# An attention loop between two layers of experts: the values' product taken for two blocks of queries at once, and the normalised input kept in memory

## The reference, cut to what matters

```python
x = x + 0.5 * _ffn_ref(_layernorm(x), controller, f1, bias, f2)
h = _layernorm(x)
Q, K, V = proj(h, Wq, bq), proj(h, Wk, bk), proj(h, Wv, bv)   # 16 heads of 64
rel_emb = rel_table[clip(i - j + 1023, 0, 2046)]
scores = (Q @ K.T + einsum('bhid,ijd->bhij', Q, rel_emb)) / 8
out = softmax(scores) @ V                                     # per head
x = x + out.transpose(0, 2, 1, 3).reshape(b, n, e) @ Wo.T + bo
x = x + 0.5 * _ffn_ref(_layernorm(x), controller, f1, bias, f2)
```

## Time and profile before

| | us |
|---|---|
| median of 3 runs | 3956.51 |
| lowest and highest | 3954.49, 4080.84 |
| the profiled execution | 3966.11 |
| its span, slowest core (core 1) | 3964.1 |
| spans of all cores | 3927.9 to 3964.1 |

### The profile page before, as it was taken

One profiled execution on the slowest core, in us unless ns is written; L12 is line 12 of the kernel. 1 busy time (PEld: TensorE's weight loads), 2 busy tenths in 40 slices (PEclk: granted clock), 3 DMA queues, 4 the chain that ended last, 5 costly groups with the idle time before them and its releaser, 6 DMA issues.

```text
span 3964.1 us, 80834 instructions; the slowest of 8 cores (3927.9 to 3964.1 us)
## 1 busy us (share of the span) xinstructions
PE 3500.4 (88%) x29664; PEld 2215.0 (56%) x29664; DVE 2097.3 (53%) x2703; ACT 1561.0 (39%) x2013; POOL 187.9 (5%) x289
## 2 busy tenths in 40 slices
PE   6988469999999999999999999999987789988842
PEld 4776134565566566566557557556654545567610
DVE  4333223666666666666666666666675733333311
ACT  3222122544554554554454454455454411122200
POOL 0000000000000000000000000000000000000001
PEclk8799687999999999999999999999998989999965
DMA  4557883564565565465466456456468711156697
GB/s 135 170 188 248 308 257 118 180 200 162 171 208 171 165 206 178 158 203 189 157 193 197 150 184 208 156 173 212 153 188 248 222 55 64 59 178 211 222 320 264
DMA packets 248833, 736.25 MB, mean 186 GB/s; under 512 B 16656, under 2 KB 66320, under 8 KB 240272
## 3 DMA queue, kind: packets, MB, share of 16 engines
q1 hardware_dynamic: 178448, 401.82, 30.7%
q0 software_dynamic: 63680, 317.74, 24.3%
q10 hardware_dynamic: 6336, 11.54, 1.3%
HBM read 405.05 MB, written 325.98 MB: 184 GB/s over the span
## 4 chain that ended last, share of the span: by engine, by line
PE 75%; DMA 13%; ACT 4%; issue 4%; DVE 3%; SPq 0%; POOL 0%; ACTq 0%; DVEq 0%; POOLq 0%
PE PS L158 65%; PE PS L155 10%; DMA out<-SCR 3%; DMA SCR<-f2r 3%; ACT SCR L981 3%; DMA xs<-SCR 3%; DMA SCR<-qsl 1%; DMA SCR<-x 1%; ACT SCR L919 1%; DVE SCR L978 1%; DVE SCR L888 1%; DMA qsl<-SCR 1%; DMA SCR<-itb 0%; DMA SCR<-xs 0%; DVE SCR L898 0%
## 5 line engine op out<-in xcount | busy, mean ns | idle before, releaser
L158 PE MATMUL PS<-SCR 128*64 128x128 f32 (+5 forms) x20928 | 3159.3, 393 | 282.9 <-DMA SCR<-itb 100.4
L158 PEld LDWEIGHTS PS<-SCR 128*64 128x64 f32 (+2 forms) x20928 | 1793.0, 167 | 1174.3 <-issue 1121.0
L888 DVE TENSOR_TENSOR SCR<-PS,SCR 128x1024 f32<-128x1024 f32 (+3 forms) x608 | 642.0, 1056 | 765.9 <-PE PS L158 730.8
L155 PEld LDWEIGHTS PS<-IDENT,SCR 64*128 64x128 f32 (+1 forms) x8736 | 456.5, 141 | 551.8 <-issue 528.6
L155 PE MATMUL PS<-IDENT,SCR 64*128 64x64 f32 (+1 forms) x8736 | 557.7, 236 | 159.2 <-ACT SCR L981 47.2
L898 DVE TENSOR_REDUCE SCR<-SCR 128x2 f32<-128x1024 f32 x512 | 622.5, 1216 | 26.7
L919 ACT ACTIVATE SCR<-SCR 128x2048 f32<-128x2048 f32 x256 | 510.7, 1996 | 122.8 <-DVE SCR L912 122.5
L802 ACT ACTIVATE SCR<-PS 128x1024 f32<-128x1024 f32 (+2 forms) x448 | 413.8, 924 | 259.6 <-PE PS L158 244.2
L981 ACT ACTIVATE SCR<-PS 128x1024 f32<-128x1024 f32 x256 | 262.5, 1025 | 363.8 <-PE PS L155 348.9
L978 DVE COPY SCR<-PS 128x1024 f32<-128x1024 f32 x256 | 311.1, 1215 | 24.9 <-PE PS L155 23.1
L943 ACT ACTIVATE SCR<-PS 128x128 f32<-128x128 f32 x128 | 35.6, 278 | 526.9 <-PE PS L155 517.3
(11 more groups left out here) (47 smaller groups left out, 616.6 us busy)
## 6 DMA issues: line engine op xcount, KB each, us to landing
qsl<-SCR SPq DMA_DIRECT2D x320, 512.0 KB, 4.8
itb<-SCR POOLq DMA_DIRECT2D x64, 1024.0 KB, 13.3
SCR<-itb SPq DMA_DIRECT2D x32, 2048.0 KB, 27.0
SCR<-f1p SPq DMA_DIRECT2D x64, 512.0 KB, 9.1
SCR<-f2r SPq DMA_DIRECT2D x64, 512.0 KB, 12.4
SCR<-qsl POOLq DMA_DIRECT2D x16, 2048.0 KB, 10.7
SCR<-qsl POOLq DMA_DIRECT2D x16, 1920.0 KB, 10.3
SCR<-qsl POOLq DMA_DIRECT2D x16, 1792.0 KB, 10.4
```

The lines of the kernel that those rows point to most:

```text
L155: return do("tensor", lambda e: e.matmul(out, lhsT, rhs, start=start, stop=stop, is_transpose=True), sig)
L158: return do("tensor", lambda e: e.matmul(out, lhsT, rhs, start=start, stop=stop), sig)
L888: e.tensor_tensor(sr(n, a0, [[1, w]]), pap(BK_C + a0 - j0, [[512, 2], [1, w]]), in1, ALU.add))
```

## The change

- **Values for two blocks.** `emit_pv` runs for odd blocks only and takes the block before along: 256 moving columns instead of 128, half of the groups. The transposed probabilities of the even block are kept whole (`PTE`, four groups), those of the odd one in two places (`PTO`). Reciprocals have a place for each of the two, and VectorE multiplies 256 columns at once.
- **h in memory.** h is laid out in four chunks of 512 rows (16 KB a partition each) and stored to `hts`. In the loop only two chunks are in SBUF; the projections of a pair go chunk by chunk (`order`), and after Q of its first and its second chunk `load_chunk` loads the other two in their places, in four transfers of 512 KB in the next four steps.
- **Q has two buffers**, so all 48 pieces of a pair run in the pair before.
- **Pieces** come in the order K, V, Q for each chunk. A step without a product of values has one piece, a step with one has one every second time.
- **Last results through memory.** The last pair's results go to `aofm` too. `prefetch` loads the first half (16 transfers) and the weights (16); the second half is loaded after the barrier, and the first two tiles of the output product start with the first half meanwhile.

The diff, cut to its core:

```diff
             for eng in Bld.ENGS:
-                barrier(eng)
+                barrier(eng, () if attn is None or eng in ("sync", "gpsimd")
+                        else ("aow", "aox"))
...
+
+                a_ld = []
+
+                def load_ao(part):
+                    for m in range(4, 8):
+                        tok = dma("sync",
+                                  ap(attn["aof"] + 2048 * m + 512 * part,
+                                     [[1, 512]]),
+                                  AP(aofm.tensor, 128 * m * S + 512 * part,
+                                     [[S, 128], [1, 512]]), LXS[part])
+                    a_ld.append(tok)
+
+                load_ao(0)
                 for t in range(2):
                     x_ld.append(dma("sync", ap(XT[t], [[1, 1024]]),
                                     src_hbm[128 * t:128 * (t + 1), :],
                                     ("xta", "xtb")[t]))
                 bo_ld = dma("sync", ap(BO, [[1, 1024]]), borep[:, :], "sx")
                 ct_ld = dma("sync", ap(CT, [[1, 1024]]), ctrlc[:, :], "ld")
+                for part in range(1, 4):
+                    load_ao(part)
             dma("sync", ap(FB, [[1, 32]]), f1bs[:, :], "ld")
...
+                o_k, o_t = {}, {}
+
+                def emit_o(t, ms):
+                    if ms[0] == 0:
+                        o_k[t] = next_pair()
+                        wt("tensor", pair_free[o_k[t]])
+                    if ms[-1] == 7 and t % 4 == 0:
+                        wt("tensor", a_ld[t // 4])
+                    for nb in range(2):
+                        bank = 1024 * o_k[t] + 512 * nb
+                        for m in ms:
+                            o_t[t] = mm(PS[:, bank:bank + 512],
+                                        ap(AOF + 2048 * m + 128 * t,
+                                           [[1, 128]]),
+                                        ap(WO[m] + 512 * nb, [[1, 512]]),
+                                        m == 0, m == 7,
+                                        sig=(nb == 1 and m == 7))
+
+
+                emit_o(0, range(4))
+                emit_o(1, range(4))
                 for t in range(NT):
-                    k = next_pair()
...
-            PT = (3072, 4096)
+            PTE, PTO = HBASE + 8192, (HBASE + 14336, HBASE + 15360)
...
-            QT = XA + 12288
+            QT = (XA + 12288, HBASE + 12288)
...
+            hbuf = [HBASE + 4096 * i for i in range(4)]
+            h_ready = [None] * 4
+            loads = []
...
+            def load_chunk(nb, done):
+
+                new, sem = (nb + 2) % 4, ("hca", "hcb")[nb % 2]
+                hbuf[new] = hbuf[nb]
+                h_ready[new] = (sem, b.cnt[sem] + 64)
+
+                def part(i, base=hbuf[nb]):
+                    if i == 0:
+                        wt("sync", done, hs_tok["a"], hs_tok["b"])
+                    dma("sync", ap(base + 1024 * i, [[1, 1024]]),
+                        hts[128 * new:128 * (new + 1),
+                            1024 * i:1024 * (i + 1)], sem)
+                loads.extend(lambda i=i: part(i) for i in range(4))
+
+            def pieces(p, j, nb):
+                last = j == 3 and p + 1 < NPAIR
...
-                        yield piece
+                for part in range(4):
+                    def piece(part=part):
+                        tok = proj_qk_piece(p, QT[p % 2], WQ, BQS, 0.125,
+                                            state["wq"], nb, part)
+                        if tok:
+                            state["q"][p % 2][nb] = state["pj"]
+                        if tok and last:
+                            wt("sync", tok)
+                            state["wq"] = load_w(wqt, WQ, p + 1, "wqa")
+                        if tok and p > 0 and j < 2:
+                            load_chunk(nb, tok)
+                    yield piece
...
+            def order(p):
+                return (2, 3, 0, 1) if p > 0 and p % 2 == 0 else (0, 1, 2, 3)
...
 
                 wt("tensor", z_tok[n], pv_free[0], rz_tok[0])
-                tok = mm(PS[:, BK_PV + 128:BK_PV + 256], ap(RB, [[1, 128]]),
+                rz = BK_PV + 256 + 128 * (n % 2)
...
-                slot = g % 2
+                dst = PTE + 1024 * g if n % 2 == 0 else PTO[g % 2]
                 eng = "vector" if g in (0, 3) else "scalar"
-                wt(eng, tok, pt_free[slot])
...
             def emit_pv(n, g):
                 p, q = n // 16, n % 16
-                wt("tensor", pt_tok[(n, g)], state["v"][p % 2])
+                even, odd = PTE + 1024 * g, PTO[g % 2]
+                wt("tensor", pt_tok[(n - 1, g)], pt_tok[(n, g)],
+                   state["v"][p % 2])
...
                     for h in range(2):
-                        tok = mm(pap(BK_PV, [[1, 128]], 64 * h, 64),
+                        tok = mm(pap(BK_PV, [[1, 256]], 64 * h, 64),
                                  ap(VT[p % 2] + 128 * kc + 64 * h, [[1, 64]]),
-                                 ap(PT[g % 2] + 256 * h + 64 * k,
-                                    [[512, 2], [1, 64]]),
+                                 ap(even + 256 * h + 64 * k,
+                                    [[odd - even, 2], [512, 2], [1, 64]]),
                                  kc == 0, kc == 15,
                                  sig=(k == 3 and h == 1))
-                pt_free[g % 2] = tok
+                pt_free[even] = pt_free[odd] = tok
...
-                        dst = AOF + 2048 * p + 128 * q
-                    elif q % 4 == 0:
+                    wt("vector", tok, rz_tok[0])
+                    dst = AOT + 512 * slot + 128 * (q % 4 - 1)
+                    if q % 4 == 1:
                         wt("vector", ao_tok[slot])
                     pv_free[0] = do("vector", lambda e: e.tensor_tensor(
-                        ap(dst, [[1, 128]]), PS[:, BK_PV:BK_PV + 128],
-                        ap(RZ, [[1, 128]]), ALU.mult))
-                    if q % 4 == 3 and n < LAST:
+                        ap(dst, [[1, 256]]), PS[:, BK_PV:BK_PV + 256],
+                        ap(RZ, [[1, 256]]), ALU.mult))
+                    if q % 4 == 3:
                         wt("gpsimd", pv_free[0])
...
+            def store_chunk(nb, which):
+                wt("gpsimd", h_ready[nb])
+                hs_tok[which] = dma(
+                    "gpsimd", hts[128 * nb:128 * (nb + 1), :],
+                    ap(HBASE + 4096 * nb, [[1, 4096]]), "hs" + which)
...
+                    todo.extend(pieces(0, t // 4, t // 4))
+                    if t >= 8:
+                        store_chunk(t // 4, "b")
...
+            store_chunk(0, "a")
+            store_chunk(1, "a")
+            wt("scalar", hs_tok["b"])
+            wt("vector", hs_tok["b"])
...
-                if i < 28:
+                if i < 16:
                     m, part = i // 4, i % 4
                     dma("scalar", ap(AOF + 2048 * m + 512 * part, [[1, 512]]),
                         AP(aofm.tensor, 128 * m * S + 512 * part,
                            [[S, 128], [1, 512]]), "af")
-                elif i < 44:
-                    m, part = (i - 28) // 2, i % 2
+                elif i < 32:
...
+                    for piece in queue:
+                        piece()
...
+                        for j, nb in enumerate(order(p + 1)):
+                            queue += pieces(p + 1, j, nb)
...
-
-                    target = max(-(-len(queue) * (4 * q + c + 1) // 64),
-                                 min(len(queue), 4 * q + c + 1, 4))
-                    while done < target:
-                        queue[done]()
-                        done += 1
-                    if tr >= 1:
+                    if loads:
+                        loads.pop(0)()
+
+                    values = tr >= 1 and (tr - 1) // 4 % 2 == 1
+                    due += 1 if values else 2
+                    while due >= 2:
+                        due -= 2
+                        if queue:
+                            queue.pop(0)()
+                    if values:
                         emit_pv((tr - 1) // 4, (tr - 1) % 4)
```

More of the change, by code:

```diff
@@ L354, in emit_logits @@
                 wt("vector", v)
+                if attn is not None and ch == 0:
+                    wt("vector", *attn["ao"])
                 prm_t[ch] = do("vector", lambda e: e.tensor_tensor(
@@ L401, in after @@
                         emit_pt(t // 2 - 1)
-                for t in range(NT):
-                    k = next_pair()
[L405 to L412, removed]
+                o_k, o_t = {}, {}
[16 more added lines that the diff above has]
+                emit_o(1, range(4))
+                for t in range(NT):
+                    emit_o(t, range(8) if t >= 2 else range(4, 8))
+                    k, tok = o_k[t], o_t[t]
                     xo = ap(XT[t % 2], [[1, 1024]])
@@ L710, in proj_v_piece @@
                 return tok
[L712 to L719, removed]
-                            if tok and nb == 3 and p + 1 < NPAIR:
```

(20 more changed lines are left out.)

88 lines of the change are left out of this document (34 added, 54 removed).

## The result

The medians of four executions of each are 4034.3 us for the changed kernel and 3995.0 for the kernel before. That leaves three of the changed kernel (4015.1, 4029.4 and 4039.2 us) and two of the kernel before (3954.5 and 3956.5). The ratio is 1.018, with a 95% interval from 1.011 to 1.026. The interval lies above 1, so the change made the kernel slower; whether by 2% it does not settle. The forecast was 3912 us with a range to 3955: wrong in size and in sign.

What follows compares the result with a forecast made beforehand. The prediction took the loop to be bound by TensorE's own stream. Terms -34 - 49 - 8 + 17 + 10 + 2 + 5 + 1 + 5 + 7 = -44 us took the median of 3956.5 to 3912 us, range 3862 to 3955.

Steps and rivals of the forecast that it cites:

- The waits: Attention loop: TensorE's waits for ScalarE's copy go, -49 us, and for VectorE's copy, -8; new waits add +17 and +10.
- The term that was +17 us: Loop blocks: late VectorE in first steps and exponentials delaying eviction of positions, 0.15 us a block, between 0 and 0.45.
- The wait for the reciprocals: First product of an odd block follows the transposed reciprocals with no piece between: 0.18 us each, +10 us.
- The wide product: Values' product in the loop: four groups of 1.96 us replace eight of 1.10 in two blocks, -34 us.
- the rival of the weight loads: Values' product with 256 columns is bound by weight loads and stays at 1.10 us: 3766 us, chance 3%.
- The middle pair of 310 us: Loop: a middle pair of heads should take 310 us instead of 318.
- Pieces moved: Q's last quarter no longer waits: pair 0 +8 us, pair 7 -8 with +2 of waits returning; +2 us in all.
- the last pair: Pair 7: only values stand between transposes, so steps without them wait for the copy as before; 0.3 a block, +5 us.
- The input from memory: Storing chunks of h costs +1 us; 14 chunk loads in the loop slow position scores, 0.35 us a burst, +5 us.
- The collision rival: Loop: each of 14 chunk-load bursts makes a block's scores late by 5.5 us, +77 instead of +5: 3984 us, chance 12%.
- The end of the loop: After the last exponentials: four products twice as wide at the lower clock, +7 us; last result through memory 0, or +3.
- the clock: Rival: the granted clock falls over 112 blocks, +365 us, giving 4277 us; chance 3%.

Runs made afterwards that it cites:

- kernel 5: Changed kernel with the 32 copies of Q from PSUM made by VectorE instead of ScalarE, order K, V, Q kept; 3924.1 us.
- Kernels 1: Changed kernel with each chunk's pieces in the order K, Q, V instead of K, V, Q, chunk loads following the last V piece; 3949.4 us.
- kernel 7: Changed kernel in the order K, Q, V, with the first pair's pieces begun two later; ratio 0.992 against the kernel before, interval 0.988 to 0.995.
- kernel 4: Changed kernel with a block's exponentials issued behind the fourth step's piece of projection instead of ahead of it; 3947.7 us.
- 2: Changed kernel, order of pieces unchanged, with pieces two ahead from the second pair on; 3984.0 us.
- 6: Kernel before the change, with its free step moved from the fourth to the second of each block; 4055.0 us.
- Kernel 9: As kernel 7, with the wide product written as two products of 128 columns in the same step; 4146.8 us, granted clock 0.81 to 0.83 for whole pairs.
- kernel 3: Changed kernel without the 56 transfers that bring chunks of h back; 4046.4 us.
- kernel 8: As kernel 7, without the 56 transfers that bring chunks of h back; middle pairs 310.4 to 311.4 us on cores 0 to 3.

## Why the prediction was wrong

**The step that failed** is in the part "The waits", its sentence on what is late next. I asked what the exponentials of 4 us hold up and named one thing, the eviction of positions (up to 0.5 us). I did not ask it of the other instruction that the new rule puts behind them, ScalarE's copy of a projection. In before the fourth step was the free one, so the earlier trace rows could not show it; the code could: one place in PSUM for pieces, a copy on ScalarE behind `emit_softmax`, a next piece one step on. The term that was +17 us should have had a collision for every chunk: 77 us of waits and the lower clock after them, together (327.6 - 310.9) x 6, about 100 us (means of all cores of after and of kernel 5). From the traces it was to be worked out: 0.5 us to the exponentials, 4.1 for both, 0.7 for the copy, less the 2.3 us or so until the next piece. Kernels 1 and 7 take it away by the order of the pieces, 4 by the order in the queue, 5 by the engine, and all land at 310 to 314 us in nearly all middle pairs; 2 does it by the phase, at a price of its own; 6 brings it about without the change. That is shown, not only argued. What the clock adds can be estimated from blocks in the same place of a pair, all cores of after. Behind stands of 3.0 us the fourth block of a pair takes 20.5 us where the clock did not fall (17 times) and 22.1 where it fell for 3.4 us (28 times). Behind stands of 3.4 us the last block takes 20.9 us without a fall (3 times), 22.1 with one of 3.4 us (17 times) and 23.6 with one of 6.8 us (20 times). So a fall costs an estimated 1.2 to 1.6 or 2.7 us, and the 19 falls of core 1 some 35 of its 102 us.

**The rest of "The waits"** held. The waits for ScalarE's copy went. Without the collision (kernels 1, 4, 5 and 7, the slowest core of each) there remain 22 to 26 us for VectorE's copy and ScalarE's copies of position products (L1033, L854 and L860 in after) in 96 blocks, 0.25 us a block where I had 0.15. The wait for the reciprocals is 8.5 us in 47, 0.18 each, as taken from the earlier trace rows.

**The wide product.** Groups take 1.95 us (1.96 forecast) and records 385 ns; columns set it, so the rival of the weight loads is refuted. Here the records of core 1, pairs 1 to 6:
```profile
L160 PE MATMUL PS<-SCR 128*128 128x512 f32 x756 | 399.9, 654 | 77.0 <-ACT SCR L726 77.0
L160 PE MATMUL PS<-SCR 128*64 128x256 f32 x3084 | 375.4, 385 | 8.6 <-ACT SCR L998 8.6
```
(I had written 0.46 us for the mean of a record. That mean was never derived, and was wrong.) The middle pair of 310 us came out at 310.2 to 311.5 in kernels 5 and 7: the sum of gain, waits and residuals was right but for the collision. Kernel 9 says that little of the gain is the width's.

**Pieces moved** and **the last pair.** My terms come to -8 us for pair 0, its four added pieces included. On core 1 it gained 9.4, but some of that is the clock's: at its start cores 0 to 3 of before ran at a granted clock of 0.81 for 41 to 60 us and took 321 to 324 us, cores 4 to 7 never did and took 316 to 318. On cores 4 and 5, which never were at 0.81 in this pair in either kernel, it went from 316.4 and 316.3 to 312.7 and 311.9, some 4 us with the one stand in it; kernel 7, which has no such stand, takes 308.0, and that is the 8. The last 15 blocks cost 6.9 us more, where I had +5 and a return of 2, less 8 for four pieces, so -1. The clock there is 0.91 against 0.95; no kernel shows why, and this miss of 8 us stays open.

**The input from memory.** +5 us was 0 as far as can be seen: kernel 3 beside after, kernel 8 beside 7. The collision rival (3984 us) ended on the right side of before by luck, since its loads collide with nothing. The median issue-to-landing time did grow, from 4.8 and 10.7 us to
```profile
SCR<-hts SPq DMA_DIRECT2D x56, 512.0 KB, 7.2
qsl<-SCR SPq DMA_DIRECT2D x320, 512.0 KB, 5.8
...
SCR<-qsl POOLq DMA_DIRECT2D x16, 2048.0 KB, 11.2
```
which is 1.5 us in 21 of room; in the middle pairs of core 1 VectorE's additions never wait for a read.

**The end of the loop.** +7 us for four wide products at the lower clock was +0.7 (core 1, from the last exponentials to the output product):
```profile
3243.61 3.68 PE L160 MATMUL PS<-SCR 128*64 128x256 f32 x16 [1.76 <-DVE SCR L1033]
...
3249.37 1.95 PE L160 MATMUL PS<-SCR 128*64 128x256 f32 x16 [1.43 <-ACT SCR L1036]
...
3253.39 1.95 PE L160 MATMUL PS<-SCR 128*64 128x256 f32 x16 [1.43 <-ACT SCR L1036]
...
3257.64 1.95 PE L160 MATMUL PS<-SCR 128*64 128x256 f32 x16 [1.66 <-DVE SCR L1033]
```
The first takes the 3.68 us that I gave each; the other three run at the upper level and take what narrow ones took at the lower. The output product cost nothing that can be seen, as said.

**The chances.** 0.95 on faster or the same came from bounds taken for costs that I had listed. The range had no room for one that I had not. "A middle pair above 315 us" was the sign that I named for being wrong, and it is what the profile shows. Of the rivals, the clock did fall, but on core 1 in 19 short stretches at stands and not from a denser stream: in kernel 5, without them, pairs 1 to 5 kept 1.00 on all cores. The prediction said that the rows of this loop do not agree with a clock of 13/16 (0.81). That holds for the middle pairs that it read. But 0.81 does occur in this dense loop: at the start of pair 0 in before, and over whole pairs in the run of kernel 9. What brings it about no run here tells.

**A rule beside these rows.** On core 5 the copy began at 1701.15, 4.5 us behind the end of its piece at 1696.64. The Trainium skill, "PSUM — Partial Sum Buffer", section "Engine vs sequencer instructions", says that the queues of ScalarE, VectorE and GpSimd are strictly first in, first out; the trace agrees. Moving one `emit` call across the piece (kernel 4) was worth some 15 us a pair.

## What to carry to other kernels

When a change moves work to another step, list for that step every instruction it issues on each engine and what stands ahead of it in that engine's queue, not only what the moved work takes from the engine that bounds the kernel; a copy of 0.67 us behind 4.1 us of exponentials costs TensorE 3 to 4 us when the next writer of the same PSUM place comes one step on. Count such schedules with their periods (here 16 steps against 12 pieces): a collision once a period doesn't show on a page that says 9 in every slice, but it shows at once in the durations of single blocks, and a part of the kernel with another phase (pair 0) is an experiment for nothing. Short stands can cost twice, since the clock is lower behind most of them.

## What the runs showed of the hardware

A stand of 3.0 to 3.9 us of a TensorE that was busy all around it could drop the granted clock from 1.00 to 0.50 for 3.4 or 6.8 us (at 19 of 23 stands on core 1 in 1968 us; four records of 512 columns took 3.34 us instead of 1.98). Stands of 3.0 us occur with and without a fall. I had expected the clock to react only to sparse phases such as the last pair. The Trainium skill, "TensorE: Matmul & The Clock Gate", section "The HAM clock gate", calls the throttled level the default, which activity releases; the trace agrees for the 19 falls, and why four stands had none it does not show.

At the end of the loop the clock rose during or right after one product of 3.68 us and stayed up through three more with waits of 1.4 to 1.7 us between, where four narrow products with the same waits stayed at the lower level. So the wide form, though it has as many columns in all, costs nothing there. Why the clock rose for the one and not for the other no run here tells.
